# DLRM tower on one core: the order of TensorE's layers and products rewritten, `keep_busy` matmuls added, and one table split moved

## The reference, cut to what matters

```python
e = stack([tbl_f[ids[:, f]] for f in range(26)], axis=1)       # 512 x 26 x 128
c = concatenate([dense[:, None, :], e], axis=1)                # 512 x 27 x 128
g = einsum('bfd,bgd->bfg', c, c)                               # 27 x 27 products per sample
z = concatenate([dense, g[:, iu, ju]], axis=1)                 # 128 + 351 columns
h = concatenate([z, dense], axis=1)                            # 607 columns
h = maximum(h @ W_top1 + b_top1, 0)                            # 512
h = maximum(h @ W_top2 + b_top2, 0)                            # 256
y = h @ W_top3                                                 # 1
```

## Time and profile before

| | |
|---|---|
| median of three executions | 117.59 us (116.9 to 119.23) |
| the profiled execution, its own time | 117.61 us |
| its span, first to last instruction | 115.8 us |
| outside the span | 1.81 us |
| mean granted TensorE clock | 0.941 |
| last product of the last tile (gram) ends | 103.2 us |
| last gather issued / landed | 91.8 / 93.8 us |

### The profile page before, as it was taken

One profiled execution on the slowest core, in us unless ns is written; L12 is line 12 of the kernel. 1 busy time (PEld: TensorE's weight loads), 2 busy tenths in 40 slices (PEclk: granted clock), 3 DMA queues, 4 the chain that ended last, 5 costly groups with the idle time before them and its releaser, 6 DMA issues.

```text
span 115.8 us, 3417 instructions
## 1 busy us (share of the span) xinstructions
PE 101.3 (87%) x1510; PEld 86.1 (74%) x1510; DVE 65.1 (56%) x94; ACT 57.3 (50%) x83; POOL 70.7 (61%) x72
## 2 busy tenths in 40 slices
PE   4999977999999999998795399999998458997992
PEld 4687844886886888886685299899987358997881
DVE  4499896888989995476916480369000622035200
ACT  4359594998939957434560002345736411223042
POOL 3777778687888777787777777777776600000000
PEclk9999999999999999999999955999999965699999
DMA  1899998989998311211222221211212200000000
GB/s 30 267 240 248 239 255 236 232 184 259 247 303 243 121 48 45 54 45 45 71 51 51 65 54 45 69 50 51 59 54 51 59 14 6 0 6 0 6 0 1
DMA packets 4925, 11.89 MB, mean 103 GB/s; under 512 B 1875, under 2 KB 1875, under 8 KB 4910
## 3 DMA queue, kind: packets, MB, share of 16 engines
q1 hardware_dynamic: 2862, 7.47, 24.8%
q0 software_dynamic: 2048, 4.20, 14.6%
HBM read 11.66 MB, written 0.00 MB: 101 GB/s over the span
## 4 chain that ended last, share of the span: by engine, by line
PE 77%; POOL 6%; issue 6%; DVE 4%; DMA 2%; ACT 2%; POOLq 0%; DVEq 0%; ACTq 0%
PE gram_ps L450 32%; PE mlp_ps L520 11%; PE gram_ps L501 9%; POOL rows L202 6%; PE tr_ps L487 5%; PE gram_ps L545 3%; PE mlp_ps L446 3%; DMA rows<-in_tbl,ids_sb 2%; PE gram_ps L578 2%; DVE table_lo L341 2%; PE gram_ps L573 2%; PE mlp_ps L516 2%; PE mlp_ps L545 1%; PE gram_ps L511 1%; PE tr_ps L520 1%
## 5 line engine op out<-in xcount | busy, mean ns | idle before, releaser
L202 POOL DMA_INDIRECT rows<-in_tbl,ids_sb x64 | 69.8, 1091 | 20.4 <-issue 18.9
L348 DVE TENSOR_SCALAR onehot<-ids_all,row_no 125x1024 fp32r<-125x1024 f32 x37 | 27.7, 757 | 7.3 <-PE gram_ps L450 6.7
L450 PE MATMUL gram_ps<-onehot,table_hi 125*128 125x512 f32 x74 | 29.2, 411 | 1.4 <-DVE table_lo L341 1.4
L450 PE MATMUL gram_ps<-onehot,table_lo 125*128 125x512 f32 x74 | 27.8, 391 | 0.0
L254 ACT COPY featT<-tr_ps 128x512 f32<-128x512 f32 x16 | 16.3, 1073 | 12.2 <-PE tr_ps L487 12.2
L450 PEld LDWEIGHTS gram_ps<-onehot,table_hi 125*128 125x128 f32 x74 | 14.0, 192 | 6.1 <-issue 3.6
L355 DVE STREAM_TRANSPOSE gramT<-gram_ps 128x864 f32<-128x864 f32 x4 | 4.3, 1083 | 24.9 <-PE gram_ps L501 24.9
L501 PE MATMUL gram_ps<-featT 128*32 128x27 f32 x1024 | 13.9, 202 | 5.0 <-issue 3.7
L501 PEld LDWEIGHTS gram_ps<-featT 128*32 128x32 f32 x1024 | 12.0, 117 | 7.4 <-issue 6.3
L450 PEld LDWEIGHTS gram_ps<-onehot,table_lo 125*128 125x128 f32 x74 | 14.0, 190 | 2.6
L520 PE MATMUL mlp_ps<-pairsT,w1p_sb 117*128 117x128 f32 x72 | 12.4, 349 | 0.9 <-DVE pairsT L376 0.9
(11 more groups left out here) (61 smaller groups left out, 91.5 us busy)
## 6 DMA issues: line engine op xcount, KB each, us to landing
table_sb<-in_tbl SPq DMA_DIRECT2D x6, 448.0 KB
table_sb<-in_tbl SPq DMA_DIRECT2D x2, 560.0 KB
rows<-in_tbl,ids_sb POOLq DMA_INDIRECT x64, 4.4
table_sb<-in_tbl SPq DMA_DIRECT2D x4, 224.0 KB
w1p_sb<-in_w_pairs SPq DMA_DIRECT2D x1, 702.0 KB
w1d_sb<-in_w_dense SPq DMA_DIRECT2D x1, 512.0 KB, 9.5
w_sb<-in_w SPq DMA_DIRECT2D x1, 512.0 KB, 13.3
table_sb<-in_tbl SPq DMA_DIRECT2D x6, 52.0 KB
```

Source lines behind the costliest of these rows:

```text
L202: pool.indirect_dma_start(out=rows[:, t % ROWS, f, :], out_offset=None, in_=tables[f][:, :], in_offset=bass.IndirectOffsetOnAxis(ap=ids_sb ...
L348: nc.vector.tensor_scalar(onehot[0:KR, n % OH, :, :], ids_all[0:KR, p % 2, :, :], row_no[0:KR, kinds.index(LK[p]), k:k + 1], None, ALU.is_ ...
L450: return nc.tensor.matmul(gram_ps[:, p % 2, m, :], part[0:KR, p % 2, m, k, :], rows_of_k[0:KR, m, :], start=start, stop=stop)
```

## The change

PE's order is rewritten, `keep_busy` matmuls are added, and three smaller things move.

- Start: `WARM` is 5, its matmuls read the constant column `one` instead of the identity, and so wait for `one_ready` rather than `ident_ready`.
- DVE: `low_part(1, 0)` stands before the one-hots of pair 1 and `low_part(1, 1)` before its third (before: ahead of the third and the fourth). The sum `w1x` stands before the three joins instead of behind them.
- PE and ACT: the layers of tile 2 are placed between and before the groups of tile 3, ahead of both halves of `gram(3)`; both halves of `gram(2)` stand close together.
- `keep_busy`: `keep_busy(n, place)` issues n matmuls of 128 x 128 on the identity: 3 and 3 around `turn_pairs(2)`, 8 before `turn_features(3, 3)`, 5 before the last `turn_pairs`.
- End: the four dense products of the last tile stand around the halves of `gram(3)`; `turn_pairs(LAST)` is split so that its first two thirds need only the first two thirds of the pairs, and the last third is turned behind the first third of layer 1.

```diff
-    WARM, WARM_ON = 4, 6
+    WARM, WARM_ON = 5, 6
...
             for p in range(1, NP):
+                if p == 1:
+                    low_part(1, 0)
                 dve.wait_ge(ids_ready, p + 1)
                 for k in range(LK[p] - 1):
-                    if p == 1 and k in (2, 3):
-                        low_part(1, k - 2)
+                    if p == 1 and k == 2:
+                        low_part(1, 1)
...
+            def keep_busy(n, place):
+
+                for i in range(n):
+                    nc.tensor.matmul(place, ident[:, :], ident[:, :], start=True, stop=True)
...
-            def turn_pairs(t):
-                pe.wait_ge(gramT_ready, 2 * (t + 1))
+            def turn_pairs(t, cs=range(NKP)):
+                if t < LAST:
+                    pe.wait_ge(gramT_ready, 2 * (t + 1))
                 flat = pairs[:, t % 2, :, :].rearrange("p f k -> p (f k)")
-                for c in range(NKP):
+                for c in cs:
                     pe.wait_ge(pairs_ready, NKP * t + c + 1)
+                    if t == LAST and c == 1:
+                        pe.wait_ge(gramT_ready, 2 * (t + 1))
...
+            pe.wait_ge(one_ready, 1)
+            ones = bass.AP(one[:, :].tensor, one[:, :].offset, [list(one[:, :].ap[0]), [0, P]])
+            for i in range(WARM):
+                nc.tensor.matmul(gram_ps[:, 1, 1, 0:P], ones, ones, start=True, stop=True)
             pe.wait_ge(ident_ready, 1)
-            for i in range(WARM):
-                nc.tensor.matmul(gram_ps[:, 1, 1, 0:P], ident[:, :], ident[:, :], start=True, stop=True)
...
             gram(1, (2, 3))
-            turn_features(2, 0)
             pe.wait_ge(w2_in, 16)
             layer2(0)
+            turn_features(2, 0)
             layer1_start(1)
             turn_pairs(1)
             turn_features(2, 1)
             layer3(0)
+            turn_features(2, 2)
             layer1(1)
-            turn_features(2, 2)
             turn_features(2, 3)
-            layer1_start(2)
             layer2(1)
             gram(2, (0, 1))
             layer3(1)
+            gram(2, (2, 3))
+            layer1_start(2)
             turn_features(3, 0)
+            keep_busy(3, gram_ps[:, 1, 1, 0:P])
+            turn_pairs(2)
+            keep_busy(3, gram_ps[:, 1, 1, 0:P])
+            layer1(2)
             turn_features(3, 1)
-            gram(2, (2, 3))
+            layer2(2)
             turn_features(3, 2)
+            layer3(2)
+            keep_busy(8, mlp_ps[:, 0, 0:P])
             turn_features(3, 3)
-            turn_pairs(2)
+            pe.wait_ge(tr_stored, TILES * NG - 1)
+            layer1_dense(LAST, 0)
             gram(3, (0, 1))
-            layer1(2)
+            layer1_dense(LAST, 1)
+            pe.wait_ge(y_ready, LAST)
+            layer1_dense(LAST, 2)
             gram(3, (2, 3))
-            layer2(2)
-            layer3(2)
-            pe.wait_ge(y_ready, LAST)
-            for j in range(J1):
-                layer1_dense(LAST, j)
-            turn_pairs(LAST)
-            layer1_last(LAST)
+            layer1_dense(LAST, 3)
+            keep_busy(5, mlp_ps[:, 0, 0:P])
+            turn_pairs(LAST, (0, 1))
+            layer1_last(LAST, (0,))
+            turn_pairs(LAST, (2,))
+            layer1_last(LAST, (1, 2))
             layer2_last(LAST)
             layer3(LAST)
```

More of the change, by code:

```diff
@@ L306, in _ @@
             hidden1(0, (0, 1, 2, 3))
+            hidden2(0)
             features(2, 0)
-            hidden2(0)
             features(2, 1)
             result(0)
+            features(2, 2)
             hidden1(1, (0, 1, 2, 3))
-            features(2, 2)
             features(2, 3)
@@ L316, in _ @@
             features(3, 0)
+            hidden1(2, (0, 1, 2, 3))
             features(3, 1)
+            hidden2(2)
             features(3, 2)
+            result(2)
             features(3, 3)
-            hidden1(2, (0, 1, 2, 3))
-            hidden2(2)
-            result(2)
             hidden1(3, (0, 1, 2, 3))
@@ L418, in _ @@
                     onehots(p, k)
+            dve.wait_ge(w1d_in, 16)
+            nc.vector.tensor_tensor(w1x, w1d_sb[:, 0, :], w1d_sb[:, 1, :], ALU.add).then_inc(w1x_ready, 1)
             join(0, slice(0, NJ - 2), NL - 2)
@@ L421, in _ @@
             join(1, slice(0, NJ), NL)
-            dve.wait_ge(w1d_in, 16)
-            nc.vector.tensor_tensor(w1x, w1d_sb[:, 0, :], w1d_sb[:, 1, :], ALU.add).then_inc(w1x_ready, 1)
             arrange_pairs(0)
@@ L536, in layer1, with layer1_last @@
                         layer1_pairs(t, j, c)
-            def layer1_last(t):
-                for c in range(NKP):
+            def layer1_last(t, cs):
+                for c in cs:
                     pe.wait_ge(pairsT_ready, NKP * t + c + 1)
@@ L576, in _ @@
             spread(0)
-            for i in range(WARM_ON):
-                nc.tensor.matmul(gram_ps[:, 1, 1, 0:P], ident[:, :], ident[:, :], start=True, stop=True)
+            keep_busy(WARM_ON, gram_ps[:, 1, 1, 0:P])
             for p in range(NP):
```

## The result

The changed kernel takes 122.47 us (median of four executions, 121.14 to 123.06), the kernel before 117.25 beside it. The ratio is 1.043, with a 95% interval of 1.029 to 1.058: slower by over 2%. The forecast was 116.9, no change; the range ended at 120.3. The profiled execution has a span of 120.3 us against 115.8.

A forecast was written before the change was run, and what follows sets the result against it. It took lookups on PE, then gathers, then PE's tail as bounds. The old span 115.8, less 1.65 in the tail, plus 104.15 - 103.24 for later products, gave 115.06, with 1.81 more 116.9 us; range 113.4 to 120.3.

The forecast's parts named there:

- What bounds the kernel before: PE's lookups to 54 us, gathers with PE slack to 94, then a tail of 22.0 us set by PE.
- That PE would become the bound: At the last group: PE never waits for rows, which have been there since 93.8; its fillers end at 98.49.
- Start: Lookups of pair 1: PE's pause ends at 17.05 instead of 18.09, and the 1.04 us arrive at the products.
- First pass and middle: Products through gram(2): old gaps 0.36 and 2.21 stay, full clock, 1.74 us block wait in gram(2), ending at 86.67.
- Fillers: Around turn_pairs(2) the two sets of three are free; the eight before the last group cost 1.96 us.
- Last products: Both halves of gram(3) and two dense products: end at 104.15, against 103.16 unhindered.
- 2.76 us a block: In gram(3): estimated spacing of PE's instruction blocks without gathers, 3.83 x 0.72; the last block begins at 103.98.
- My upper end: In gram(3): at 3.83 us a block the last could begin at 105.66, and the end is 105.8.
- Tail: Behind gram(3): layer 1 of the last tile starts at 106.2 in old time instead of 107.99; gain 1.65 us.
- The clock rival: Layer 1 of tile 0: the clock falls again and now counts, plus 2.75 us, 119.6 to 121.3; chance 0.22.
- The blocks cost nothing more: In gram(2) and gram(3): instruction supply keeps pace, so 1.74 and 1.0 us go, time 114.2; chance 0.24.
- The sum: Whole kernel: span 115.8 - 1.65 + (104.15 - 103.24) = 115.06, plus 1.81, time 116.9.

The follow-up runs named there:

- e5: Kernel before with DVE's new order of the table remainders and eight keep_busy matmuls ahead of its last group; 114.85 us, ratio 0.995.
- e3: Kernel before with only PE's new start (five first matmuls on the constant column); 116.17 us, ratio 0.984.
- e8: Kernel before with DVE's new order, the split last turn_pairs and two of the last tile's dense products drawn ahead; 115.8 us.
- e11: Kernel before with only DVE's new order of the table remainders, run again over twelve executions; 114.83 us, ratio 0.989.
- e2: Changed kernel with PE's old start (four matmuls on the identity); 125.37 us.
- e1: Changed kernel without the eight keep_busy matmuls before the last group; 121.3 us.
- e9: Changed kernel with twelve one-column matmuls (48 more PE instructions) in front of the first three fillers; 123.33 us.
- e7: Changed kernel with all four keep_busy calls taken out; 121.95 us.
- e12: Changed kernel run again with no edit, six executions; 122.38 us, beside 115.76 for the kernel before.
- e6: Changed kernel without the eight fillers, with layers 2 and 3 of tile 2 between the halves of gram(3); 120.5 us, ratio 1.040.
- e4: Kernel before with only DVE's new order of the table remainders; 113.88 us, ratio 0.977.

## Why the prediction was wrong, point by point

**What bounds the kernel before** was read right for its profile: in e5 PE waits for rows behind 1.95 us of fillers. But the slack is small and not always there; in the profiles of e3, e8 and e11 PE gets to the last group after its rows. **That PE would become the bound** was right as well: no wait for rows, the last group turned at 99.50 against 98.49 forecast.

**Start.** Wrong by 2.4 us in the profiled execution: the pause ended at 19.48 and not at 17.05, and gram(0) began at 57.0 instead of 54.6. I took the clock's rise at 8 us for a property of the program; it came near 14 in four of fourteen profiles, under both starts. In the other cases the second half of the step failed too: in e2 the pause ended at 17.26, and the gain was gone at the third pair, behind ACT and its tables (e1 and e11 have that wait as well, 0.5 and 1.6 us). In no profile with DVE's new order did gram(0) begin earlier than 55.4 us, against 55.6 in the kernel before. That PE's row stands at 9 behind the pause was evidence of the old order only.

**First pass and middle.** The full clock in layer 1 of tile 0 was right here (2.92 us). The gaps of 1.67 and 0.72 us were smaller than the 2.21 and 1.74 of the sum, and the one of 0.36 didn't come at all. Together they took back most of the start's error: gram(2) ended at 87.5, forecast 86.67. The second gap was where I had counted it, after 97 records of the second half; the forecast was 95.

**Fillers.** Right: the first two sets cost nothing, the eight ran with the rows long landed, at 97.64.

**Last products. This is the step that failed most.** The step is the term "2.76 us a block", which set the end of gram(3) at 104.15. It was sized by the speed of a gram half, and gave 0.99 us of gaps; the trace has 2.07 + 1.22 = 3.3. The end of gram(3) came 4.3 us late, of which 1.0 were brought along (the last group at 99.50 against 98.49) and 3.2 arose here (8.9 us from the last group to that end, against 5.7). Two things were wrong in it. Without gathers the spacing is hardly shorter: 108.02 - 104.56 = 3.46 us, in e1 106.74 - 103.29 = 3.45, against 3.83 with them. And the request for a block is held back while PE stands in a wait: the border in the fillers was passed at about 99.4, the wait for ACT's store ended at 101.2, the packet moved at 102.1, and the next block could begin only at 104.56. e9 moves that border ahead of the wait and the gap is gone; there the stretch from the last group to the end takes 17.1 us, close to the 16.6 of the forecast. My upper end, 3.83 for each block, gave 105.8 for a measured 108.4, since it lacked this second part.

**Tail.** The split worked: layer 1 of the last tile began 3.5 us behind the products (108.4 to 111.96) instead of 4.8. But the clock fell to half from 106.1 to 112.9, behind the gaps, which cost about 1 us: the five fillers took 2.34 us, in e9 at full clock 1.28. So the span ended 11.9 us behind gram(3) and not 10.9; in e9 it ended 10.8 behind. Among the seven profiles with the new order the clock fell this late in four, the three with a gap of over 2 us in gram(3) (the changed kernel twice, e2) and e7.

**The rivals.** The clock rival named the wrong place: not layer 1 of tile 0 in the profiled execution, but the tail. Its argument, that falls now count in full, isn't settled: e12's two ends give 0.49 us for each us at half clock, all ten executions 0.34, the kernel before 0.35. "The blocks cost nothing more" is refuted: each of the seven profiles with the new order has a gap in gram(2) (0.55 to 1.42 us), and all but e6, where slow matmuls stand between the halves, have one in gram(3). The Trainium skill (Runtime: NRT & Kernel Launch, "Instruction fetch mechanics") says that crossing a block border is mostly hidden. The traces agree where slow work follows the border, as in e6, and not in runs of small matmuls, where single gaps reach 2.69 us (e2).

**The sum** was short because it took the favourable value in three places at once: an early clock, quick blocks, no fall in the tail. In the profiled execution they came to 1.0 us ahead of the last group, 3.2 in the products and 1.0 in the tail, together the 5.2 between the forecast span of 115.06 and the measured 120.3. The size of the blocks was an error and so, in part, was the start; the late rise and the fall in the tail are what other executions of the same kernels have or don't have, and can't be told from draws. The tail's gain is also stated as 1.65 us where its own terms give 107.99 - 106.2 - 0.11 = 1.7, which changes nothing.

What stays open is why e2 had such low clocks, and how the 4.5 to 6.6 us at equal clock divide. e1, with the eight fillers and one gap of gram(3) gone, has 118.06 at the clock 0.985: 3.6 us are still there, and 2.9 in e6. Beside the gaps that are left, the layers moved ahead of the last group are the likely part (in e1 it is turned at 97.78 against 92.86 in e4, both at 0.985), but these weren't taken apart further.

The best version that ran is DVE's order alone in the kernel before (e4, e11): 113.9 and 114.8 us.

## What to carry to other kernels

Before work is moved ahead of a transfer, add up whether the engine gets there later than the transfer does; slack that looks wasted in a profile may be what absorbs clock falls and late starts. Keep long runs of tiny matmuls apart with slow ones, and count PE's instructions: a block border in front of a wait, with dense work behind it, is the worst place for it. Fillers are free only in a gap that remains when they are in place; that they gain time no run here shows.

## What the runs showed that was not expected

- Behind a block of some 256 PE instructions that PE had to wait for, the next one began 3.45 us later with the DMA engines nearly idle (3.46 in the changed kernel, 3.45 in e1, 3.73 in e2), and not 2.76. It isn't a fixed distance: in e9, where the block before began without a wait near 105.3 us (counted back from the gap, an estimate), it was about 3.1.
- A wait of PE behind a border delays the fetch to its end: 5.2 us from border to border in the changed kernel, of which 2.7 passed before the packet moved; behind the next border, at 104.56, without a wait, it moved after 1.1 us (a packet at 105.6 to 105.8).
- The clock can fall even in the dense lookups. In e3 it stood at half from 28.8 to 35.5 us, behind a single pause of 1.61 us, and PE was busy throughout; e2 has a pause of 1.56 us in the same place and no fall behind it:

```profile
28.80:35.50 6.70, 6.70 (x15) 4.36 (x15) 2.80 (x4) 5.38 (x7) 5.45 (x5) 0.50 1.04 251
```

- A matmul of 128 x 128 weights with a single moving column in float32 takes 2.74 / 12 = 0.23 us, nearly as much as one with 128 columns (0.245).
